# Gated values kept patch by patch, and the w_in matmuls of a step run over all four quarters

## The chip, the cores and the metric

One Trainium2 chip, one core. The metric is the device time of one launch in microseconds (us); the kernel before has a median of 3460.51 us over 3 runs (3444.41 to 3466.08). TensorE is called PE (its weight loads PEld), VectorE DVE, ScalarE ACT, GpSimd POOL, SyncE SP. All data is fp32. SBUF holds 128 partitions; PSUM has 8 banks of 512 fp32 words in each.

## The reference

The input is x of 32 images, 32 channels, 96 x 96 pixels. The program is two parts, one after the other:

```python
x = x + experts(groupnorm(x))      # gate picks 3 of 6 experts an image; each: 3x3 depthwise conv, relu, 3x3 depthwise conv
x = x + fft_conv(groupnorm(x))

def fft_conv(x, w_in, dw_k, fft_filter, w_out):
    x = einsum('oc,bchw->bohw', w_in, x)          # 32 -> 170 channels
    xp = 8x8 patches of x                          # 144 patches an image
    x = irfft2(rfft2(xp) * fft_filter)             # per channel, inside each patch
    y = depthwise 3x3 conv(x, dw_k)                # across patch borders too
    y1, y2 = y[:, :85], y[:, 85:]
    return einsum('oc,bchw->bohw', w_out, gelu(y1) * y2)
```

Only the second part (from about 1180 us of the profile on) is touched by the change.

## The kernel before, in words

**Layout.** In the second part an image lies as 4 quarters of rows (q = 0 to 3) of 32 channels on the 128 partitions. Its 144 patches are 36 to a quarter. After w_in a patch's 64 pixels are on 64 partitions and there are two halves h (partitions 0 to 63 and 64 to 127) that hold different channels: `hidden_patches` (U) is [128, 88 channels, 144 patches]. The filter and the 3x3 kernel are folded, once, into tables of 64 x 64 for each channel (`channel_tables`, line 965), so the FFT, the filter and the convolution are matmuls of one channel's table with its 144 patches.

**Two stages an image.** The main loop (lines 1314 to 1328 for PE, 1382 to 1398 for DVE, 1192 to 1208 for ACT) has for each image k a *first stage* and then eight *sets*.

The first stage has NW = 9 steps. In step v, PE does w_in of image k for 4 patches of each quarter (`w_in_step`, line 1234, matmuls at line 1245: 32 calls of 32 rows x 64 columns, moving 88; the quarter picks the array's row group and PSUM bank 4 + q, h picks the column half) and then w_out of image k - 1 (`w_out_step`, line 1299, matmuls at line 1309: 16 calls of 128 rows x 32 columns, moving 128). Each matmul call shows as two matmul and two weight-load records, since fp32 is done in two passes. w_in goes by pairs of quarters: pair 0 into banks 4 and 5, then pair 1 into banks 6 and 7. ACT copies each pair out to U (`w_in_copy`, line 1148, copies at line 1153) and frees its banks for the same pair of the next step (semaphores `s_w`, `s_we[pair]`). DVE transposes the gated values of image k - 1 in 32 x 32 blocks so that channels lie on partitions (`transposes`, line 1359, two instructions of 128 x 512 at line 1369), and adds the result of w_out of the step before to the image (`residual`, line 1380). The `channels_first` buffers and the PSUM banks of w_out (2 and 3) are double.

The eight sets hold 3, 3, 3, 3, 3, 3, 2, 2 slots of channel pairs. For set S PE runs `border(S+2)` (line 1263), `hidden(S)` (line 1280, the patch's own part) and `add_neighbours(S)` (line 1295, what comes over the patch borders, brought by DMAs from `border` to `neighbours`, lines 1076 and 1190). ACT then takes `gelu` of one half of the channels (line 1180) and DVE multiplies it with the other half into `gated` (`gate`, line 1356), once for the even and once for the odd slots (odd = 0, 1). `hidden(S+1)` writes the same PSUM banks 0 to 3, so it waits for both gates of set S (`need(pe, s_m, 2 * S)`, line 1270). Each engine runs its queue in the program's order.

**`gated`** (gt, line 967) is [128, 44 slots, 144 patches]. A gate of 3 slots writes 3 runs of 144 adjacent words; a transpose reads 32 slots of one patch, with a step of 144 words from element to element, patch after patch.

Four older pieces of code serve as measures. Line 252 copies `taps` tables to SBUF with a step of 32 words from element to element of its inner loop; line 249 copies `tables` with a step of 54 words; line 1347 (and 1174 on ACT) writes `channel_tables` with a step of 128 words. Line 554 (first convolution of the experts) has 24 matmul calls of 32 rows x 64 columns that run over four row groups and two column halves in the innermost loops, moving 288; line 568 (second convolution) has 12 calls of 128 rows x 32 columns over four column groups, moving 288.

The instruction memory is refilled by DMA while the program runs; the page's DMA queue 8, kind "instruction", has 586 packets and 9.60 MB.

Of the kernel before, what the change touches and what calls it, by code (L numbers as in the profile page):

```python
# [13 lines left out]
P = 128  # L14
# [825 lines left out]
NQUAD = 4  # L840
# [107 lines left out]
def filter_part(nc, x1, norm2, w_in, dw_k, filt, w_out, out):  # L948
# [9 lines left out]
    with ExitStack() as ctx:  # L958
        def sb(name, shape):
            return ctx.enter_context(nc.sbuf_tensor(name, shape, F32))  # L960
# [3 lines left out]

        tbl = sb("channel_tables", [P, NCH, 2 * NV])
        U = sb("hidden_patches", [P, NCH, NPC])
        gt = sb("gated", [P, NT4, NPC])
        be = [sb(f"border{i}", [P, RUN + 2 * EDGE]) for i in range(2)]
        bd = [sb(f"neighbours{i}", [P, RUN]) for i in range(2)]
        ct = [sb(f"channels_first{i}", [P, 2 * 512]) for i in range(2)]  # L970
# [53 lines left out]
        def need(eng, s, value):  # L1024
            if value > 0:
                eng.wait_ge(s, value)
# [184 lines left out]
        def _(pe):  # L1211
# [19 lines left out]
                                  mid[half(h), j:j + n, NCH * g:NCH * g + NCH], start=True, stop=True)  # L1231
                    last.then_inc(s_x, 1)

            def w_in_step(k, v, pair):

                if v == 0 and pair == 0:
                    pe.wait_ge(s_xn, k + 1)
                need(pe, s_we[pair], NW * k + v)
                if k == 0 and v == 0:
                    pe.wait_ge(s_xe[pair], NGX)  # L1240
                for i in range(WSTEP):
                    for q in (2 * pair, 2 * pair + 1):
                        cq = slice(C * q, C * q + C)
                        for h in range(2):
                            last = MM(ps[half(h), 4 + q, i * NCH:(i + 1) * NCH], xn[cq, (WSTEP * v + i) * NV:(WSTEP * v + i + 1) * NV], wi[cq, NCH * h:NCH * h + NCH],  # L1245
                                      start=True, stop=True)
                last.then_inc(s_w, 1)

            def border(S):

# [63 lines left out]
            for k in range(B + 1):  # L1314
                for v in range(NW):
                    if k < B:
                        w_in_step(k, v, 0)
                        w_in_step(k, v, 1)
                    if k > 0:
                        w_out_step(k - 1, v)  # L1320
                if k < B:
                    border(NSETS * k)
                    border(NSETS * k + 1)
                    for s in range(NSETS):
                        if s + 2 < NSETS:
                            border(NSETS * k + s + 2)
                        hidden(NSETS * k + s)
                        add_neighbours(NSETS * k + s)

        @block.vector  # L1330
        def _(dve):
# [17 lines left out]
            def gate(S, odd):  # L1349
                k, s = divmod(S, NSETS)  # L1350
                n = SETS[s]
                dve.wait_ge(s_g, 2 * S + odd + 1)
                if s == 0:
                    need(dve, s_te, NW * k)
                o = gt.rearrange("p (t s) n -> p t s n", s=2)[:, CUT[s]:CUT[s + 1], odd, :]
                TT(o, gl[odd][:, 0:n * NPC].rearrange("p (t m) -> p t m", m=NPC),  # L1356
                   ps[:, 2 * odd + 1, 0:n * NPC].rearrange("p (t m) -> p t m", m=NPC), ALU.mult).then_inc(s_m, 1)

            def transposes(k, v):

                j = NW * k + v
                if v == 0:
                    dve.wait_ge(s_m, 2 * NSETS * (k + 1))
                need(dve, s_wo, j - 1)
                t = ct[j % 2].rearrange("p (s q i n) -> p s q i n", s=2, q=NQUAD, i=WSTEP)
                for s in range(2):
                    first = s * (NT4 - SB)
                    g = gt[:, first:first + SB, :].rearrange("p t (q i) -> p q i t", q=NQUAD)[:, :, WSTEP * v:WSTEP * v + WSTEP, :]
                    last = nc.vector.transpose(t[:, s], g)  # L1369
                last.then_inc(s_te, 1)  # L1370

# [57 lines left out]
```

## Time and profile before

| | |
|---|---|
| median of 3 runs | 3460.51 us |
| profiled execution, first to last instruction | 3457.4 us |
| PE matmul busy | 2908.9 us (84%) |
| DVE busy | 1847.5 us (53%) |
| ACT busy | 1311.5 us (38%) |
| mean granted TensorE clock | 0.953 |

The page gives no time for the profiled execution but its span; the median lies 3.1 us above it. Busy times overlap, so no one of them is the time: what counts is which engine waits for which, stage by stage. A granted clock of 1 is 2.4 GHz, 0.5 is 1.2 GHz. In a timeline row "x64" counts records, so 64 matmul records are 32 calls. "Idle before <-issue" is time in which an engine waited for nothing that the profile shows.

### The profile page before, as it was taken

The page shows a single profiled execution, that of the slowest core. Times are in us where ns is not written, and L with a number is a line of the kernel's source. Part 1 is how long each engine was busy: PE and PEld are TensorE (multiplying, and loading weights), DVE is VectorE, ACT ScalarE, POOL GpSimd, SP SyncE. Part 2 cuts the span into 40 slices and gives each one's busy share as a digit, 9 for nine tenths or more (in the row PEclk, how much of TensorE's full clock was granted, in tenths as well). Part 3 has the DMA queues.
Part 4 walks back from the last instruction along what each step waited for, and adds up shares of the span by engine and source line. Part 5 has one row for each costly group of instructions (what it writes and reads, how often), then busy time and mean ns, then how long its engine had stood idle before and what let it go on. Part 6 is the DMA issues. An engine that isn't in the chain of part 4 may idle for free.

```text
span 3457.4 us, 164388 instructions
## 1 busy us (share of the span) xinstructions
PE 2908.9 (84%) x74374; PEld 2020.6 (58%) x74374; DVE 1847.5 (53%) x4198; ACT 1311.5 (38%) x2217; POOL 253.1 (7%) x274
## 2 busy tenths in 40 slices
PE   4699999999996788888888888888888888888887
PEld 4355554555453666666666666666656666666665
DVE  3356565565652245554556555655555555555555
ACT  1234444444342233343434343433433333443332
POOL 2011111111110200000000000000000000000000
PEclk9899999999998599999999999999998999999999
DMA  6578778787764334334443444334433444334433
GB/s 126 124 170 172 164 169 170 172 171 165 165 144 69 32 100 111 95 93 104 117 106 89 107 119 105 89 99 105 116 97 89 105 115 112 89 99 113 113 92 84
DMA packets 451958, 404.16 MB, mean 117 GB/s; under 512 B 404172, under 2 KB 404478, under 8 KB 447497
## 3 DMA queue, kind: packets, MB, share of 16 engines
q1 hardware_dynamic: 446030, 376.93, 47.5%
q10 hardware_dynamic: 5228, 16.70, 1.4%
q8 instruction: 586, 9.60, 1.2%
q14 instruction: 114, 0.93, 0.1%
HBM read 165.77 MB, written 78.16 MB: 71 GB/s over the span
## 4 chain that ended last, share of the span: by engine, by line
PE 49%; DVE 6%; issue 5%; ACT 3%; DMA 3%; ACTq 2%; SPq 1%; POOL 0%; DVEq 0%; POOLq 0%
PE ps L1295 12%; PE ps L1245 10%; PE ps L1280 10%; PE ps L1309 9%; PE ps L1263 8%; DMA neighbours<-border 3%; DVE gated L1356 3%; ACT gelu L1180 2%; DVE channels_first L1369 2%; ACTq L1190 2%; ACT hidden_patches L1153 1%; DVE border L1163 1%; SPq L1052 1%; ACT border L1163 0%; DMA x_normed<-in_L_conv_w_in_dram 0%
## 5 line engine op out<-in xcount | busy, mean ns | idle before, releaser
L1356 DVE TENSOR_TENSOR gated<-gelu,ps 128x432 f32<-128x432 f32 (+1 forms) x512 | 289.3, 567 | 555.8 <-ACT gelu L1180 529.7
L449 ACT ACTIVATE hidden<-ps,hidden_scale 128x576 f32<-128x576 f32 x512 | 351.7, 738 | 614.5 <-PE ps L554 614.5
L1369 DVE STREAM_TRANSPOSE channels_first<-gated 128x512 f32<-128x512 f32 x576 | 571.3, 1043 | 1.1
L1153 ACT COPY hidden_patches<-ps 128x704 f32<-128x704 f32 x576 | 406.5, 749 | 434.3 <-PE ps L1245 434.2
L1280 PE MATMUL ps<-hidden_patches,channel_tables 64*64 64x144 f32 x11264 | 403.4, 287 | 97.4 <-DVE gated L1356 97.4
L1263 PE MATMUL ps<-hidden_patches,channel_tables 64*64 64x144 f32 x11264 | 405.7, 287 | 90.2 <-DVE border L1163 84.8
L568 PE MATMUL ps<-hidden,taps 128*32 128x288 f32 x6144 | 437.3, 417 | 43.1 <-DMA taps<-conv_tables 29.7
L1245 PE MATMUL ps<-w_in_t,x_normed 32*64 32x88 f32 x18432 | 422.3, 259 | 54.2 <-issue 49.3
L1263 PEld LDWEIGHTS ps<-hidden_patches,channel_tables 64*64 64x64 f32 x11264 | 359.4, 134 | 184.6 <-ACT border L1163 114.7
L1163 ACT COPY border<-ps 128x432 f32<-128x432 f32 (+1 forms) x512 | 226.4, 495 | 618.9 <-DVE border L1163 216.9
L554 PE MATMUL ps<-x_rows,taps 32*64 32x288 f32 x12288 | 455.0, 415 | 2.5 <-issue 1.3
L1163 DVE COPY border<-ps 128x432 f32<-128x432 f32 (+1 forms) x512 | 267.9, 565 | 320.1 <-PE ps L1263 160.0
L1245 PEld LDWEIGHTS ps<-w_in_t,x_normed 32*64 32x64 f32 x18432 | 356.7, 145 | 138.8 <-issue 134.4
L1295 PE MATMUL ps<-neighbours,select 64*64 64x432 f32 (+1 forms) x4096 | 400.6, 505 | 43.8 <-DMA neighbours<-border 23.0
L1280 PEld LDWEIGHTS ps<-hidden_patches,channel_tables 64*64 64x64 f32 x11264 | 338.4, 133 | 166.1 <-DVE gated L1356 156.7
L1309 PE MATMUL ps<-channels_first,w_out_t 128*32 128x128 f32 x9216 | 359.2, 296 | 84.9 <-DVE channels_first L1369 68.4
L554 PEld LDWEIGHTS ps<-x_rows,taps 32*64 32x64 f32 x12288 | 271.5, 133 | 179.5 <-issue 94.9
L1180 ACT ACTIVATE gelu<-ps 128x432 f32<-128x432 f32 (+1 forms) x512 | 255.9, 502 | 310.9 <-PE ps L1295 302.7
L1309 PEld LDWEIGHTS ps<-channels_first,w_out_t 128*32 128x32 f32 x9216 | 260.6, 117 | 135.6 <-DVE channels_first L1369 76.8
L790 DVE SCALAR_TENSOR_TENSOR x_image<-ps,out_bias,x_image 128x288 f32<-128x288 f32 x256 | 130.9, 511 | 380.1 <-PE ps L568 378.8
L568 PEld LDWEIGHTS ps<-hidden,taps 128*32 128x32 f32 x6144 | 176.7, 110 | 249.5 <-issue 124.2
L1295 PEld LDWEIGHTS ps<-neighbours,select 64*64 64x64 f32 x4096 | 134.5, 132 | 201.5 <-PE ps L1280 105.4
(147 smaller groups left out, 1328.7 us busy)
## 6 DMA issues: line engine op xcount, KB each, us to landing
neighbours<-border SPq DMA_DIRECT2D x1024, 126.8 KB
taps<-conv_tables SPq DMA_DIRECT2D x192, 216.0 KB
x_image<-in_x_dram SPq DMA_DIRECT2D x128, 288.0 KB, 5.8
x<-x_image SPq DMA_DIRECT2D x128, 288.0 KB, 4.7
x_image<-x SPq DMA_DIRECT2D x384, 96.0 KB
out_dram<-x_image SPq DMA_DIRECT2D x384, 96.0 KB, 2.0
x_rows<-in_x_dram SPq DMA_DIRECT2D x512, 60.0 KB
neighbours<-border ACTq DMA_DIRECT2D x1024, 15.8 KB
```

The lines of the kernel that those rows point to most:

```text
L449: A(hid[T % 3][:, 2 * h:2 * h + 2, :, 1:1 + W], ps1[:, 2 * h:2 * h + 2, 0:XB * W].rearrange("p c (k w) -> p c k w", k=XB), ACT.Relu, scale ...
L554: last = MM(ps1[MP * u:MP * u + MP, f, 0:XB * W], t1s[n % 2][rows, j, dx, :], t[rows, j, u:NBLK:2, dx:dx + W], start=(dx == 0), stop=(dx = ...
L568: last = MM(ps2[RX * f:RX * f + RX, T % 2, 0:XB * W], t2s[n % 2][:, o:o + RX], hid[T % 3][:, f, :, dx:dx + W], start=(dx == 0), stop=(dx = ...
L1153: nc.scalar.copy(o, i).then_inc(s_we[pair], 1)
L1163: last = copy(o[:, i, 0:n, 0:NPR, 0:NPR], ps[:, 4 + i, 0:n * NPC].rearrange("p (u r c) -> p u r c", u=n, r=NPR))
L1245: last = MM(ps[half(h), 4 + q, i * NCH:(i + 1) * NCH], xn[cq, (WSTEP * v + i) * NV:(WSTEP * v + i + 1) * NV], wi[cq, NCH * h:NCH * h + NCH ...
L1263: last = MM(ps[half(h ^ y), 4 + i, o:o + NPC], tbl[half(h), j, NV:2 * NV], U[half(h), j, :], start=True, stop=True)
L1280: last = MM(ps[half(h ^ odd), i, o:o + NPC], tbl[half(h), j, 0:NV], U[half(h), j, :], start=first, stop=True, skip_group_check=not first)
L1295: last = MM(ps[half(h ^ odd), i, 0:n * NPC], sel[half(h ^ y), :], v[half(h ^ y), i, 0:n, 0:NPR, 0:NPR], start=False, stop=True, skip_group ...
L1309: last = MM(o, wo[:, b, s, :], t[:, s, P * q:P * q + P], start=(s == 0), stop=(s == 1), skip_group_check=True)
L1356: TT(o, gl[odd][:, 0:n * NPC].rearrange("p (t m) -> p t m", m=NPC), ps[:, 2 * odd + 1, 0:n * NPC].rearrange("p (t m) -> p t m", m=NPC), AL ...
L1369: last = nc.vector.transpose(t[:, s], g)
```

## The change

`gated` becomes [128, 144 patches, 44 slots]: the 44 slots of a patch are adjacent words. So the gate's inner loop over 144 patches writes with a step of 44 words, while the transposes read 32 adjacent words for each patch. Both have as many elements as before.

`w_in_step` no longer has a pair: one call does all four quarters, with q and h as the innermost loops, so that successive matmul calls go over four row groups and two column halves. It first waits until both pairs of the step before have been copied out. The two increments of `s_w` both come in the last round (i = 3), after q = 1 and after q = 3. The number and shapes of the matmuls and the copies stay the same.

```diff
--- before.py
+++ after.py
@@ -964,7 +964,7 @@
 
         tbl = sb("channel_tables", [P, NCH, 2 * NV])
         U = sb("hidden_patches", [P, NCH, NPC])
-        gt = sb("gated", [P, NT4, NPC])
+        gt = sb("gated", [P, NPC, NT4])
         be = [sb(f"border{i}", [P, RUN + 2 * EDGE]) for i in range(2)]
         bd = [sb(f"neighbours{i}", [P, RUN]) for i in range(2)]
         ct = [sb(f"channels_first{i}", [P, 2 * 512]) for i in range(2)]
@@ -1231,20 +1231,22 @@
                                   mid[half(h), j:j + n, NCH * g:NCH * g + NCH], start=True, stop=True)
                     last.then_inc(s_x, 1)
 
-            def w_in_step(k, v, pair):
-
-                if v == 0 and pair == 0:
+            def w_in_step(k, v):
+
+                if v == 0:
                     pe.wait_ge(s_xn, k + 1)
-                need(pe, s_we[pair], NW * k + v)
-                if k == 0 and v == 0:
-                    pe.wait_ge(s_xe[pair], NGX)
+                for pair in range(2):
+                    need(pe, s_we[pair], NW * k + v)
+                    if k == 0 and v == 0:
+                        pe.wait_ge(s_xe[pair], NGX)
                 for i in range(WSTEP):
-                    for q in (2 * pair, 2 * pair + 1):
+                    for q in range(NQUAD):
                         cq = slice(C * q, C * q + C)
                         for h in range(2):
                             last = MM(ps[half(h), 4 + q, i * NCH:(i + 1) * NCH], xn[cq, (WSTEP * v + i) * NV:(WSTEP * v + i + 1) * NV], wi[cq, NCH * h:NCH * h + NCH],
                                       start=True, stop=True)
-                last.then_inc(s_w, 1)
+                        if i == WSTEP - 1 and q % 2 == 1:
+                            last.then_inc(s_w, 1)
 
             def border(S):
 
@@ -1314,8 +1316,7 @@
             for k in range(B + 1):
                 for v in range(NW):
                     if k < B:
-                        w_in_step(k, v, 0)
-                        w_in_step(k, v, 1)
+                        w_in_step(k, v)
                     if k > 0:
                         w_out_step(k - 1, v)
                 if k < B:
@@ -1352,7 +1353,7 @@
                 dve.wait_ge(s_g, 2 * S + odd + 1)
                 if s == 0:
                     need(dve, s_te, NW * k)
-                o = gt.rearrange("p (t s) n -> p t s n", s=2)[:, CUT[s]:CUT[s + 1], odd, :]
+                o = gt.rearrange("p n (t s) -> p t s n", s=2)[:, CUT[s]:CUT[s + 1], odd, :]
                 TT(o, gl[odd][:, 0:n * NPC].rearrange("p (t m) -> p t m", m=NPC),
                    ps[:, 2 * odd + 1, 0:n * NPC].rearrange("p (t m) -> p t m", m=NPC), ALU.mult).then_inc(s_m, 1)
 
@@ -1365,7 +1366,7 @@
                 t = ct[j % 2].rearrange("p (s q i n) -> p s q i n", s=2, q=NQUAD, i=WSTEP)
                 for s in range(2):
                     first = s * (NT4 - SB)
-                    g = gt[:, first:first + SB, :].rearrange("p t (q i) -> p q i t", q=NQUAD)[:, :, WSTEP * v:WSTEP * v + WSTEP, :]
+                    g = gt[:, :, first:first + SB].rearrange("p (q i) t -> p q i t", q=NQUAD)[:, :, WSTEP * v:WSTEP * v + WSTEP, :]
                     last = nc.vector.transpose(t[:, s], g)
                 last.then_inc(s_te, 1)
```

## Rows read from the trace of the kernel before

**Rows 1.** The page's part 4, the chain that ended last, by engine.

```profile
PE 49%; DVE 6%; issue 5%; ACT 3%; DMA 3%; ACTq 2%; SPq 1%; POOL 0%; DVEq 0%; POOLq 0%
```

**Rows 2.** Timeline, one set of the second part: start, length (us), engine, line, what, [idle before].

```profile
2007.41 1.70 PE L1280 MATMUL ps<-hidden_patches,channel_tables 64*64 64x144 f32 x48 [0.33 <-DVE gated L1356]
2009.20 1.69 PE L1295 MATMUL ps<-neighbours,select 64*64 64x432 f32 x16
2010.22 0.53 ACT L1180 ACTIVATE gelu<-ps 128x432 f32<-128x432 f32 x1 [0.78 <-PE ps L1295]
2010.79 1.35 DVE L1356 TENSOR_TENSOR gated<-gelu,ps 128x432 f32<-128x432 f32 x2 [1.70 <-ACT gelu L1180]
2012.19 0.35 PE L1280 MATMUL ps<-hidden_patches,channel_tables 64*64 64x144 f32 x4 [0.33 <-DVE gated L1356]
```

**Rows 3.** Groups by form: busy us, mean ns | idle before. The gates.

```profile
L1356 DVE TENSOR_TENSOR gated<-gelu,ps 128x432 f32<-128x432 f32 x384 | 231.1, 604 | 387.0 <-ACT gelu L1180 364.4
L1356 DVE TENSOR_TENSOR gated<-gelu,ps 128x288 f32<-128x288 f32 x128 | 58.2, 455 | 168.8 <-ACT gelu L1180 165.3
```

**Rows 4.** Groups by form: VectorE copies whose inner loop writes with a wide step.

```profile
L252 DVE COPY taps<-ps 128x384 f32<-128x384 f32 x8 | 6.4, 804 | 21.4 <-PE ps L585 21.4
L249 DVE COPY tables<-ps 128x480 f32<-128x480 f32 x2 | 2.0, 1006 | 19.9 <-PE ps L580 19.9
L1347 DVE COPY channel_tables<-ps 128x440 f32<-128x440 f32 x6 | 6.3, 1096 | 2.8 <-PE ps L1230 2.6
```

**Rows 5.** Groups by form, the transposes.

```profile
L1369 DVE STREAM_TRANSPOSE channels_first<-gated 128x512 f32<-128x512 f32 x576 | 571.3, 1043 | 1.1
```

**Rows 6.** Timeline, two steps after the last image.

```profile
3439.29 1.95 DVE L1369 STREAM_TRANSPOSE channels_first<-gated 128x512 f32<-128x512 f32 x2
3441.47 1.95 DVE L1369 STREAM_TRANSPOSE channels_first<-gated 128x512 f32<-128x512 f32 x2
```

**Rows 7.** Timeline, one step of a first stage.

```profile
2033.01 1.24 PE L1245 MATMUL ps<-w_in_t,x_normed 32*64 32x88 f32 x64
2033.91 1.39 ACT L1153 COPY hidden_patches<-ps 128x704 f32<-128x704 f32 x2 [0.79 <-PE ps L1245]
2034.18 1.08 PE L1309 MATMUL ps<-channels_first,w_out_t 128*32 128x128 f32 x32
2035.19 1.43 PE L1245 MATMUL ps<-w_in_t,x_normed 32*64 32x88 f32 x64
```

**Rows 8.** Timeline, two issue gaps in a row in a first stage.

```profile
1415.53 0.68 PE L1245 MATMUL ps<-w_in_t,x_normed 32*64 32x88 f32 x23 [0.54 <-issue]
1418.99 0.86 PE L1309 MATMUL ps<-channels_first,w_out_t 128*32 128x128 f32 x24 [0.25 <-issue]
```

**Rows 9.** Stretches: length, busy us (instructions) by engine, clock, DMA, GB/s.

```profile
1396.61:1400.52 3.91, 3.91 (x100) 3.23 (x97) 2.64 (x4) 1.42 (x2) 0.00 (x0) 0.50 0.02 4
1745.39:1770.03 24.64, 21.48 (x868) 17.74 (x865) 21.08 (x29) 13.13 (x20) 0.00 (x0) 1.00 0.26 65
2586.40:2617.65 31.25, 26.90 (x868) 22.30 (x865) 21.25 (x28) 13.17 (x20) 0.00 (x0) 0.78 0.22 54
```

**Rows 10.** Timeline, the first stage of the first image, without w_out.

```profile
1193.81 2.12 PE L1245 MATMUL ps<-w_in_t,x_normed 32*64 32x88 f32 x64 [0.19 <-ACT hidden_patches L1153]
1195.32 1.42 ACT L1153 COPY hidden_patches<-ps 128x704 f32<-128x704 f32 x2 [0.89 <-PE ps L1245]
```

**Rows 11.** Timeline, the turn from one image's sets to the next first stage.

```profile
2023.04 0.96 DVE L1356 TENSOR_TENSOR gated<-gelu,ps 128x288 f32<-128x288 f32 x2 [2.58 <-ACT gelu L1180]
2024.04 3.85 DVE L1369 STREAM_TRANSPOSE channels_first<-gated 128x512 f32<-128x512 f32 x4
2026.09 1.08 PE L1309 MATMUL ps<-channels_first,w_out_t 128*32 128x128 f32 x32 [1.89 <-DVE channels_first L1369]
```

**Rows 12.** Timeline, experts part: four column tiles, then eight tiles.

```profile
601.74 1.66 PE L568 MATMUL ps<-hidden,taps 128*32 128x288 f32 x24
603.33 1.72 PE L554 MATMUL ps<-x_rows,taps 32*64 32x288 f32 x48
```

## The prediction

> **What bounds the kernel now.** I read first the chain of waits: PE carries 49% of it, DVE 6% [rows 1], so what PE waits for decides, stage by stage. The timeline of a set shows a closed loop. `hidden` starts at 2007.41, `add_neighbours` at 2009.20, gelu at 2010.22, the two gates from 2010.79 to 2012.14, the next `hidden` at 2012.19: 4.78 us, and PE's idle time before it is put down to the gate [rows 2]. The border matmuls that lie between don't fill it. In all 224 places where a `hidden` follows a gate within an image, it starts 0.055 us after the second gate ends, as here (2012.14 to 2012.19). So whatever a gate gets longer, the set gets longer.
>
> In the first stage a step has 64 w_in records from 2033.01, 32 w_out records from 2034.18, the next w_in at 2035.19: 2.18 us, PE without a pause. The ACT copies begin 0.90 us after w_in and take 1.39 together [rows 7]. That is PE's own pace, but few steps keep it. The 30 stages with both kinds of matmul last 24.6 (shortest) to 31.3 us (longest) [rows 9], mean 27.2, where 4.15 + 7 x 2.18 + 2.44 = 21.9 would do. Two things take the rest. First, issue gaps: from the gap's end at 1415.53 to that at 1418.99 there are 23 + 32 + 64 + 8 = 127 matmul records, each with a weight load, so 254 instructions in 3.46 us [rows 8]. Such gaps come every 254 or 255 instructions, in this stage alone, which looks like the supply of instructions; at that pace a step's 192 can't take less than 2.62 us. Second, the clock: at a granted 0.50 (1.2 GHz) a step takes 3.91 us [rows 9]. Of the 240 steps after a stage's first, 19 are wholly at that clock, 27 partly (mean 3.06), and of the others the 166 within the stage average 2.65.
>
> **The gate (added cost).** It takes 604 ns for 432 elements and 455 for 288: 1.035 ns each and 157 fixed [rows 3]. With the inner step of 44 words no row shows it. The copies with a wide inner step give, less the same 157: step 32 words (804 - 157)/384 = 1.68 ns, step 54 (1006 - 157)/480 = 1.77, step 128 (1096 - 157)/440 = 2.13 [rows 4]. The lower bound is no cost, 1.035, since those are copies and this has two sources; the upper is 2.13. I take 1.77, of the nearest step. A gate of three slots is then 157 + 432 x 1.77 = 922 ns, of two 667. The second gate now starts 1.35 - 0.60 = 0.75 us after the first (when its gelu is ready) [rows 2, 3]; back to back it would start about 0.10 before the first one's end (two transposes take 1.95, one 1.04) [rows 5, 6], so at 0.82: 0.07 later. A three-slot set grows by 0.07 + 0.32 = 0.39 us. Two-slot gates start 0.96 - 0.455 = 0.51 apart [rows 11]: 0.06 + 0.21 = 0.27. Six such sets and one before the last `hidden` make 2.61 us an image, **+84 us** for 32. The bounds: at 1.035 nothing, at 1.68 +67, at 2.13 +150. DMAs for the neighbours are two sets ahead and only get more time. The skill has a number of its own: the Trainium skill, "Vector Engine (DVE) Microarchitecture Reference", "Measured stream behaviour on trn2", gives 2.50 ns per element for a destination that steps 24 words each element and 1.71 for hops of 4 KiB. By 2.50 the gates would cost an estimated +218 us, by 1.71 about +72; the rows of this kernel lie near the lower one.
>
> **The transposes (gain, mostly covered).** 1043 ns for 512 elements is (1043 - 157)/512 = 1.73 ns each [rows 5], just what the wide steps cost above. With adjacent words I take 1.035: 157 + 530 = 0.69 us, a pair in 1.30 instead of 1.95 to 2.0. Bounds: 0.69 and 1.04. In the steps PE doesn't wait for them. They count in two places. At the turn, w_out of step 0 waits for the first pair with 1.89 us of idle PE [rows 11]: 0.66 less, 0.27 given back by the last gates, 0.39 us an image; some of that is lost again to instruction supply, so 31 x 0.26 = **-8**. After the last image the period is DVE's, 2.18 us [rows 6]; it becomes 2 x 0.6 + 0.3 = 1.5, but PE at 1.2 GHz gives some 1.7: **-5**.
>
> **w_in over four quarters.** 24 calls over eight tiles (1.72 us) take hardly longer than 12 of the same columns over four (1.66) [rows 12]; so eight tiles run side by side, and w_in of 1.17 us (2034.18 - 2033.01 [rows 7]) becomes 0.6. But PE then has nothing to do with it: the last matmul of the quarter pairs is in the eighth round of eight, as pair 0's was before, so the first copy still starts at 0.90, the second ends at 0.90 + 1.39 = 2.29, and now the next w_in waits for both, with some 0.1 us for the semaphore: **2.39 us a step where it was 2.18**. ACT's two copies, once beside the other pair's matmuls, are in series with w_in. So:
> - Warm steps: 73 of the 166 took less than 2.39; lengthening each to 2.39 costs 14 us. Where the supply of instructions sets 2.62 anyway it costs nothing, and a slower step lets it catch up: half, **+7**. The rest stay at 2.65.
> - Steps at 1.2 GHz: the first copy starts 1.51 us after w_in, both take 1.42 [rows 10], 2.98 in all, against 3.91: 19 x 0.93 + 27 x 0.36 = **-28**. Bounds: none of it, or twice, if these stretches shrink or grow.
> - First image (no w_out, 1.2 GHz): its steps of 2.31 (1193.81 to 1196.12, PE already waits for ACT there [rows 10]) become 2.98: 8 x 0.67 = **+5**.
> - The last step of a stage is bounded by the same two copies before and after: nothing.
>
> **Sum.** 84 - 8 - 5 + 7 - 28 + 5 = +55: 3457.4 + 55 = 3512, and 3.1 more for the median, **3516 us** (+1.6%). This case's own range is 3465 (gates at 1.68, the first stages 60 us better) to 3560 (first stages not better at all, gates somewhat dearer).
>
> **Rivals.**
> - *The gaps close.* If the gaps are no limit of pace but come from PE running ahead, PE's pauses for ACT would swallow them: a stage is 3.76 + 7 x 2.39 + 2.44 = 22.9, 4.3 us less than the mean, -129 for 30. With +84 for the gates: 3416, **faster**. It decides if refilling 254 instructions takes less than 2.39 x 254/192 = 3.16 us. For it: the sets, with 192 instructions in 4.78 us, have no such gaps. Against: 3.46 measured with PE waiting [rows 8]. The Trainium skill, "Runtime: NRT & Kernel Launch", "Instruction fetch mechanics", calls crossing a 16 KiB block of instructions mostly hidden; the trace disagrees, with 0.54 and 0.25 us of matmul idle at these two [rows 8]. Chance 0.12.
> - *A wide write is free for a two-source operation.* Gates as before: 3516 - 84 - 4 = 3428. Against: every wide write in the trace is slow. 0.08.
> - *The write costs as with 128 words, or more.* +150 for +84: 3582, and beyond if no row here bounds it. 0.10.
> - *The eight tiles don't run side by side with 88 columns*, since here a round is short (88 of 288 columns): w_in stays at 1.17, the first copy starts at 1.49, the step is 2.98. 166 x 0.33 = 55 instead of 7, and the 1.2 GHz steps gain nothing (+33 against the sum): 3597. 0.07.
> - *The transposes don't get faster*: 3516 + 13 = 3529, inside the forecast.
>
> **Numbers.** The forecast has 0.63. The range 3430 to 3600 leaves out most of the first rival and the far end of the third and fourth. A measurement of this kernel tells 1% from no change, here 3426 to 3495. Faster by more: 0.08 from the first rival and 0.03 from the second. Within: 0.05 from the second, 0.04 from the first, 0.14 from the low side of the forecast. Slower: 0.66.
>
> **What would show it.** Gates of 0.92 and 0.67 us with the next `hidden` still 0.06 behind them and sets of 5.17 us; transposes of 0.69; w_in records done in about 0.85 instead of 1.24; the idle time before w_in released by ACT, steps of 2.39 or more, and gaps still 254 instructions apart, 3.4 us or more. Gates at 0.60, or first stages near 23 us, would make it wrong.

## The result, and the profile after

The changed kernel takes 3545.84 us (median of 4 runs, 3534.48 to 3557.3) where the kernel before takes 3457.55 in the same comparison (4 runs): a ratio of 1.028, interval 1.0235 to 1.0326. That is slower by 88 us; the forecast was 55 slower, 3516 us. The profiled execution spans 3555.3 us, 98 more than the one before, at a mean clock of 0.962. Line numbers moved: w_in is L1246, `border` L1265, `hidden` L1282, `add_neighbours` L1297, w_out L1311, the gate L1357, the transposes L1370.

The page after, its busy times by engine and the chain of waits:

```profile
PE 2839.7 (80%) x74374; PEld 1928.9 (54%) x74374; DVE 1766.8 (50%) x4198; ACT 1310.9 (37%) x2217; POOL 253.0 (7%) x274
PE 29%; DVE 10%; ACT 10%; issue 7%; SPq 6%; DMA 5%; ACTq 1%; POOL 0%; DVEq 0%; POOLq 0%
```

PE and DVE are both busy for less time than before and the kernel is longer; PE's share of the chain fell from 49% [rows 1] to 29%, and DVE and ACT took over. So time went into waits between engines. A set (timeline of the kernel after):

```profile
2132.33 1.70 PE L1282 MATMUL ps<-hidden_patches,channel_tables 64*64 64x144 f32 x48 [0.72 <-DVE gated L1357]
2134.12 1.68 PE L1297 MATMUL ps<-neighbours,select 64*64 64x432 f32 x16
2135.14 0.53 ACT L1180 ACTIVATE gelu<-ps 128x432 f32<-128x432 f32 x1 [0.94 <-PE ps L1297]
2135.70 1.72 DVE L1357 TENSOR_TENSOR gated<-gelu,ps 128x432 f32<-128x432 f32 x2 [2.79 <-ACT gelu L1180]
2137.48 1.21 PE L1282 MATMUL ps<-hidden_patches,channel_tables 64*64 64x144 f32 x32 [1.68 <-DVE gated L1357]
```

The gates end at 2137.42 and `hidden` starts 0.06 later, as in [rows 2]; the two gates take 1.72 us where they took 1.35, and the set 5.15 where it took 4.78. The groups by form of the kernel after (busy us, mean ns | idle before) give the new durations:

```profile
L1357 DVE TENSOR_TENSOR gated<-gelu,ps 128x432 f32<-128x432 f32 x384 | 336.3, 957 | 424.6 <-ACT gelu L1180 424.6
L1357 DVE TENSOR_TENSOR gated<-gelu,ps 128x288 f32<-128x288 f32 x128 | 78.2, 685 | 174.2 <-ACT gelu L1180 174.2
L1370 DVE STREAM_TRANSPOSE channels_first<-gated 128x512 f32<-128x512 f32 x576 | 369.7, 685 | 1.1
L1246 PE MATMUL ps<-w_in_t,x_normed 32*64 32x88 f32 x18432 | 329.4, 258 | 150.6 <-ACT hidden_patches L1153 89.8 <-issue 56.5 <-POOL x_normed L1145 3.2
```

A three-slot gate went from 604 to 957 ns [rows 3], a transpose from 1043 to 685 [rows 5]. PE now idles 89.8 us before w_in for ACT's copies.

The turn, from one image's sets to the next first stage, and the step after it (timeline of the kernel after):

```profile
1479.28 1.01 PE L1246 MATMUL ps<-w_in_t,x_normed 32*64 32x88 f32 x64
1480.62 2.49 DVE L1370 STREAM_TRANSPOSE channels_first<-gated 128x512 f32<-128x512 f32 x4
1481.98 1.08 PE L1311 MATMUL ps<-channels_first,w_out_t 128*32 128x128 f32 x32 [1.69 <-DVE channels_first L1370]
1482.99 1.01 PE L1246 MATMUL ps<-w_in_t,x_normed 32*64 32x88 f32 x64
1483.93 1.08 PE L1311 MATMUL ps<-channels_first,w_out_t 128*32 128x128 f32 x32
1483.97 1.40 ACT L1153 COPY hidden_patches<-ps 128x704 f32<-128x704 f32 x2 [2.32 <-PE ps L1246]
1485.51 1.00 PE L1246 MATMUL ps<-w_in_t,x_normed 32*64 32x88 f32 x64 [0.50 <-ACT hidden_patches L1153]
```

PE waits 1.69 us at the turn for the transposes, where it waited 1.89 [rows 11]. In the step, ACT's copies start 0.98 after w_in and last 1.40, to 1485.37; the next w_in starts at 1485.51, so a step takes 2.52 us with PE idle at its end, where 2.18 was possible [rows 7]. The issue gaps are still there (timeline, further on):

```profile
1862.19 0.83 PE L1246 MATMUL ps<-w_in_t,x_normed 32*64 32x88 f32 x47 [0.50 <-ACT hidden_patches L1153]
1863.78 0.44 PE L1246 MATMUL ps<-w_in_t,x_normed 32*64 32x88 f32 x17 [0.77 <-issue]
```

What these gaps wait for can be read from the DMA packets of queue 8, kind "instruction". The page has 586 of them, each of 16,384 bytes in the trace, for 148,748 matmul and weight-load records: 254 records to a packet, which is the distance from gap to gap. In this trace 94 in 100 of the gaps over 0.3 us end between 1.1 and 1.7 us after such a packet has ended (median 1.4); with packets some 3.7 us apart, chance alone would give about 16 in 100. The next packet starts 1.4 us after the gap's end and takes 1.1 (medians). That makes a round of 3.9 us, the spacing of the gaps. The kernel before shows the same: 94 in 100, and 1.4, 1.3 and 1.1 us. So the gaps are waits for refills of the instruction memory.

The shortest first stage after an image and one of the longest (stretches; columns as in [rows 9]) lie closer together than before, where they were 24.64 and 31.25:

```profile
3388.13:3413.51 25.38, 19.67 (x868) 15.55 (x865) 16.02 (x29) 13.04 (x20) 0.00 (x0) 1.00 0.26 66
1554.95:1583.82 28.87, 21.89 (x869) 17.41 (x865) 16.02 (x29) 13.11 (x20) 0.00 (x0) 0.88 0.24 58
```

To read the runs that follow, all instructions of a trace were sorted into the 31 first stages with both kinds of matmul and the stretches between them (the rest of an image). Means in us; "warm steps" are steps 1 to 7 that lie wholly at a granted 1; "turn wait" is PE's idle time in one turn, and the median of the 31 turns is within 0.02 us of it. The medians are of all runs, the other columns of the one profiled execution, which for the kernel after was the longest of four (3557.3 us).

| kernel | median | first stage | rest of image | turn wait | at 1.2 GHz in first stages, total | warm step, mean |
|---|---|---|---|---|---|---|
| before | 3457.55 | 27.17 | 43.30 | 1.89 | 144 | 2.64 |
| after | 3545.84 | 27.16 | 46.26 | 1.69 | 63 | 2.82 |
| layout alone | 3519.14 | 26.36 | 46.49 | 1.47 | 68 | 2.70 |
| w_in order alone | 3499.67 | 27.94 | 43.46 | 2.15 | 97 | 2.85 |
| gates alone | 3576.73 | 28.07 | 46.22 | 2.14 | 186 | 2.66 |
| transposes alone | 3405.07 | 25.42 | 43.39 | 1.21 | 24 | 2.66 |
| early transposes | 3401.01 | 25.24 | 43.30 | 0.97 | 22 | 2.66 |
| later w_out | 3396.69 | 25.08 | 43.35 | 0.46 | 23 | 2.71 |
| half of the copies | 3536.27 | 26.08 | 46.62 | 1.70 | 62 | 2.69 |
| less w_out, on after | 3609.56 | 27.05 | 48.06 | 1.70 | 710 | none |
| less w_out, on transposes alone | 3339.55 | 22.29 | 44.56 | 1.21 | 413 | 1.93 |

So the 98 us of span are, in the main, the rest of 32 images, 32 x 2.96 = 95 (the last image's alone is 4.9 longer, 2 more than the others'), and the first image's stage, 27.42 for 21.58, +6. What runs before the second part took 1 us more. The first stages of the other images are unchanged as a sum, and the work after the last image's matmuls is 5.2 us shorter (20.6 for 25.7). That the stages are unchanged is two things that cancel, which the experiments separate.

### The profile page after: what moved, and what is told of

Its sections match the earlier page's. It is cut to its first block, busy times and chain, and to the rows that moved or that the text cites. A ratio compares the mean times of both kernels' runs of the same rounds, so it can differ in the third digit from the quotient of the medians.

```text
span 3555.3 us, 164645 instructions
## 1 busy us (share of the span) xinstructions
PE 2839.7 (80%) x74374; PEld 1928.9 (54%) x74374; DVE 1766.8 (50%) x4198; ACT 1310.9 (37%) x2217; POOL 253.0 (7%) x274
## 4 chain that ended last, share of the span: by engine, by line
PE 29%; DVE 10%; ACT 10%; issue 7%; SPq 6%; DMA 5%; ACTq 1%; POOL 0%; DVEq 0%; POOLq 0%
PE ps L1282 8%; DVE gated L1357 8%; PE ps L1246 8%; ACT hidden_patches L1153 7%; PE ps L1297 6%; DMA neighbours<-border 5%; SPq L1076 4%; PE ps L1311 4%; PE ps L1265 3%; ACT gelu L1180 3%; DVE channels_first L1370 1%; ACTq L1190 1%; SPq L1058 1%; DVE border L1163 1%; SPq L1052 1%
## 5 line engine op out<-in xcount | busy, mean ns | idle before, releaser
L1357 DVE TENSOR_TENSOR gated<-gelu,ps 128x432 f32<-128x432 f32 (+1 forms) x512 | 414.5, 889 | 598.8 <-ACT gelu L1180 598.8
L1282 PE MATMUL ps<-hidden_patches,channel_tables 64*64 64x144 f32 x11264 | 407.7, 289 | 166.2 <-DVE gated L1357 166.2
L1265 PE MATMUL ps<-hidden_patches,channel_tables 64*64 64x144 f32 x11264 | 404.9, 286 | 99.6 <-DVE border L1163 85.1
L1282 PEld LDWEIGHTS ps<-hidden_patches,channel_tables 64*64 64x64 f32 x11264 | 342.1, 134 | 251.3 <-DVE gated L1357 251.3
L1265 PEld LDWEIGHTS ps<-hidden_patches,channel_tables 64*64 64x64 f32 x11264 | 359.9, 134 | 193.8 <-ACT border L1163 111.7
L1246 PE MATMUL ps<-w_in_t,x_normed 32*64 32x88 f32 x18432 | 329.4, 258 | 150.6 <-ACT hidden_patches L1153 89.8
L1297 PE MATMUL ps<-neighbours,select 64*64 64x432 f32 (+1 forms) x4096 | 406.7, 512 | 46.9 <-DMA neighbours<-border 26.8
L1311 PE MATMUL ps<-channels_first,w_out_t 128*32 128x128 f32 x9216 | 342.5, 286 | 77.4 <-DVE channels_first L1370 59.3
L1246 PEld LDWEIGHTS ps<-w_in_t,x_normed 32*64 32x64 f32 x18432 | 266.2, 138 | 243.8 <-issue 129.1
L1370 DVE STREAM_TRANSPOSE channels_first<-gated 128x512 f32<-128x512 f32 x576 | 369.7, 685 | 1.1
L1311 PEld LDWEIGHTS ps<-channels_first,w_out_t 128*32 128x32 f32 x9216 | 251.4, 114 | 120.4 <-DVE channels_first L1370 66.4
L1381 DVE TENSOR_TENSOR x_image<-ps,x_image 128x256 f32<-128x256 f32 x288 | 122.2, 424 | 348.6 <-PE ps L1311 346.7
```

What stands on the lines that cost most here:

```text
L1265: last = MM(ps[half(h ^ y), 4 + i, o:o + NPC], tbl[half(h), j, NV:2 * NV], U[half(h), j, :], start=True, stop=True)
L1282: last = MM(ps[half(h ^ odd), i, o:o + NPC], tbl[half(h), j, 0:NV], U[half(h), j, :], start=first, stop=True, skip_group_check=not first)
L1297: last = MM(ps[half(h ^ odd), i, 0:n * NPC], sel[half(h ^ y), :], v[half(h ^ y), i, 0:n, 0:NPR, 0:NPR], start=False, stop=True, skip_group ...
L1311: last = MM(o, wo[:, b, s, :], t[:, s, P * q:P * q + P], start=(s == 0), stop=(s == 1), skip_group_check=True)
```

## Experiments

**Each half of the change alone.** `layout` makes the change to `gated` alone: the declaration, the gate's output view and the transposes' input view, with w_in by pairs. `order` makes the change to `w_in_step` and its call alone. Both are the parts of the diff shown above. From here on a difference in us is against the kernel before as it was timed beside each run: 11 runs, with medians of 3463.42 us for these two and the next two, 3457.81 for `early`, `half_copies` and the two with less w_out, and 3463.64 for the rest.

> The patch-by-patch layout alone (gates write with a step of 44 words, transposes read adjacent words), w_in in two pairs as before. Theory 1 (the gates carry the loss, because each set is a closed loop through the gate): gates 957 and 685 ns, sets 5.18 us apart instead of 4.78, so 2.7 us x 32 = +86 us; the shorter transposes give back about 10 at the turn and after the last image; 3458 + 76 = 3534 us. Theory 2 (the loss comes from w_in over four quarters, whose copies are now in series with it): this kernel is about 10 us faster than before, 3448. First stages near 26.7 us in theory 1.

> w_in over all four quarters alone, gated values slot by slot as before. Theory 1: w_in in 0.95 us instead of 1.17 but a floor of 2.51 us a step instead of 2.18 (first copy 0.97 after w_in, 0.64 + 0.75 for the copies, 0.14 until the next w_in); since instruction supply already makes the mean step 2.65, the 31 first stages together change by -20 to +30 us, the first image's gets 6 us longer: 3440 to 3495. Theory 2: +80 us or more, 3540. Gates 604 ns, sets 4.78 us apart in both.

`layout`: 3519.14 us, ratio 1.0151 (1.0114 to 1.0187), +56. `order`: 3499.67, ratio 1.01 (1.0066 to 1.0133), +36. They add up to 92 against 88 for both. For `layout` 3534 had been expected; `order` came out just above the 3440 to 3495 expected. PE at the turn, in `layout` and in `order`:

```profile
1473.51 1.08 PE L1309 MATMUL ps<-channels_first,w_out_t 128*32 128x128 f32 x32 [1.47 <-DVE channels_first L1369]
```

```profile
2045.96 1.94 PE L1311 MATMUL ps<-channels_first,w_out_t 128*32 128x128 f32 x32 [2.15 <-DVE channels_first L1370]
L1246 PE MATMUL ps<-w_in_t,x_normed 32*64 32x88 f32 x18432 | 334.2, 261 | 147.7 <-ACT hidden_patches L1153 87.8 <-issue 55.8 <-POOL x_normed L1145 3.2
```

The new order is not a small gain but a cost. Its w_in is done earlier, so PE waits longer at the turn (2.15 for 1.89), and w_out there then runs its 32 records in 1.94 us instead of 1.08, at the lower clock.

**Each half of the layout alone.** The memory stays the same, only one of the two views changes.

```diff
# gate_only: the gates write with a step of 44, the transposes read with 144
+ gt = sb("gated", [P, NPC, NT4])
+ o = gt.rearrange("p n (t s) -> p t s n", s=2)[:, CUT[s]:CUT[s + 1], odd, :]
+ old = gt.rearrange("p n t -> p (n t)").rearrange("p (t n) -> p t n", t=NT4)
# transposes_only: the gates as before, the transposes read adjacent words
+ new = gt.rearrange("p t n -> p (t n)").rearrange("p (n t) -> p n t", t=NT4)
```

> Only the gates write with a step of 44 words; the transposes read the same memory with a step of 144 words as before (so they take wrong values), w_in as before. Theory 1: the whole loss and a little more: +86 us, 3544; first stages as before, 27.2 us mean; transposes still 1043 ns. Theory 2: no change.

> Only the transposes read adjacent words (wrong values, since the gates write slot by slot as before), w_in as before. Theory 1: 685 ns each instead of 1043, but off the path except at the turn (0.65 us x 31, part of it lost to instruction supply) and after the last image (5 us): -10 to -25 us, 3433 to 3448. If the transposes were a limit in the steps, the first stages would fall below 25 us and the time below 3400.

`gate_only`: 3576.73 us, ratio 1.0307 (1.0267 to 1.0348), +113. `transposes_only`: 3405.07, ratio 0.9834 (0.9806 to 0.9862), -58. They add up to +55, the layout's +56. Both went further than expected (+86, and -10 to -25), because of the turn, as the rows below show. The turn in `gate_only` (timeline) and the five microseconds from 2075 (stretch):

```profile
2075.91 1.93 PE L1309 MATMUL ps<-channels_first,w_out_t 128*32 128x128 f32 x32 [2.14 <-DVE channels_first L1370]
2075.00:2080.00 5.00, 4.09 (x112) 3.48 (x116) 4.72 (x6) 0.71 (x2) 0.00 (x0) 0.66 0.00 0
```

The turn in `transposes_only` and the steps behind it:

```profile
2005.33 2.49 DVE L1370 STREAM_TRANSPOSE channels_first<-gated 128x512 f32<-128x512 f32 x4
2006.69 1.08 PE L1309 MATMUL ps<-channels_first,w_out_t 128*32 128x128 f32 x32 [1.21 <-DVE channels_first L1370]
2007.70 1.24 PE L1245 MATMUL ps<-w_in_t,x_normed 32*64 32x88 f32 x64
2008.88 1.08 PE L1309 MATMUL ps<-channels_first,w_out_t 128*32 128x128 f32 x32
2009.88 1.24 PE L1245 MATMUL ps<-w_in_t,x_normed 32*64 32x88 f32 x64
```

After 2.14 us of idle PE the clock averages 0.66 over those five microseconds; after 1.21 w_out stays at its 1.08 and the next step takes 2.18 (2007.70 to 2009.88). Over the 31 stages, time at 1.2 GHz is 24 us against 144, step 0 takes 3.46 against 4.47 and step 1 2.18 against 3.06. In kernels with w_in by pairs, waits of 1.21, 1.47, 1.89 and 2.14 go with 24, 68, 144 and 186 us at 1.2 GHz, in 4, 14, 23 and 25 of the 31 stages; with the new order, 1.69 and 2.15 with 63 and 97, in 17 and 23.

**The transposes' rate, or the wait at the turn?** `early` keeps the old layout and its slow transposes, but DVE does those of slots 0 to 31 for steps 0 and 1 before the gates of the last set.

```diff
+ def early_transposes(k):
+     dve.wait_ge(s_m, 2 * (NSETS * k + 6))
+     need(dve, s_wo, NW * k)
+     for v in range(2):
+         transpose_part(k, v, 0)
  # DVE's loop over the sets, ahead of the gates of the last one
+ if s == NSETS - 2:
+     early_transposes(k)
  # (not shown: in the first stage, steps 0 and 1 then transpose slots 12 to 43 alone)
```

> The kernel before with two transposes moved: the ones that read slots 0 to 31 for the steps 0 and 1 of the first stage run on VectorE in its pause before the gates of the last set (those slots are complete by then). All else as before. Theory 1 (PE's wait at the turn from the sets to the first stage costs twice: itself, and by the drop of the granted clock to 0.5 that follows it): the turn's idle time falls from 1.9 to about 0.9 us, step 0 from 4.47 to about 3.2, hardly any first stage at 1.2 GHz; 3463 - 65 = 3398 us. Theory 2 (the clock falls for other reasons): only the wait itself, 31 us or less: 3432 to 3450.

3401.01 us, ratio 0.984 (0.981 to 0.9869), -57. Its transposes by form, and w_out at the turn:

```profile
L1364 DVE STREAM_TRANSPOSE channels_first<-gated 128x512 f32<-128x512 f32 x576 | 578.6, 1053 | 1.1
2000.95 1.08 PE L1309 MATMUL ps<-channels_first,w_out_t 128*32 128x128 f32 x32 [0.97 <-DVE channels_first L1364]
```

With transposes of 1053 ns the gain is that of transposes of 684 ns. After the last image the faster ones save 5.6 us of their 58 (the work there takes 20.2 us for 25.7), `early` 1.7. In the first stages their rate is worth nothing beyond the turn (warm steps take 2.66 us in both kernels and 2.64 before); the wait at the turn, with the clock behind it, is worth all of it.

**Give PE something else to do at the turn.** `late` issues w_out one step later on PE, so that w_in of steps 0 and 1 come ahead of the first w_out. `late_early` has both edits.

```diff
-                    if k > 0:
-                        w_out_step(k - 1, v)
+                    if k > 0 and v > 0:
+                        w_out_step(k - 1, v - 1)
+                if k > 0:
+                    w_out_step(k - 1, NW - 1)
```

> The kernel before with PE's order in the first stage changed alone: w_out follows one step later (w_in 0, w_in 1, w_out 0, w_in 2, w_out 1, ...), all else as before, the transposes too. PE then has w_in of step 1 to do where it waited 1.9 us for the transposes. Theory 1 (that wait also brings the drop of the clock): idle time at the turn about 0.5 + 0.2 us in two pieces, hardly any first stage at 1.2 GHz, and the last two w_out cover ACT's last copies; first stages 25.0 instead of 27.2, 3458 - 68 = 3390 us. Theory 2 (clock independent of the wait): 31 x 1.3 = 40 us less at most, 3418.

> Both the later w_out and the two early transposes. If supply of instructions sets the first stages once the wait and the clock are out of the way, little more comes: 24.5 to 25 us a stage, 3375 to 3400 us, within 15 us of either alone. If the wait still counted, the two would add: 3340.

`late`: 3396.69 us, ratio 0.9805 (0.9776 to 0.9834). `late_early`: 3393.59, ratio 0.9805 (0.9773 to 0.9837): the second edit adds nothing that shows in the time, though time at 1.2 GHz in the first stages falls from 23 us to 7. Both beat both kernels. The turn in `late`:

```profile
2006.56 1.24 PE L1245 MATMUL ps<-w_in_t,x_normed 32*64 32x88 f32 x64
2007.46 1.39 ACT L1153 COPY hidden_patches<-ps 128x704 f32<-128x704 f32 x2 [0.33 <-PE ps L1245]
2007.64 3.92 DVE L1371 STREAM_TRANSPOSE channels_first<-gated 128x512 f32<-128x512 f32 x4
2008.26 1.48 PE L1245 MATMUL ps<-w_in_t,x_normed 32*64 32x88 f32 x64 [0.46 <-ACT hidden_patches L1153]
2009.72 1.08 PE L1309 MATMUL ps<-channels_first,w_out_t 128*32 128x128 f32 x32
```

PE idles 0.46 us, for ACT, and w_out follows without a wait.

**Are the issue gaps a limit of pace?** `half_copies` is the changed kernel in which ACT, from image 1 on, copies out 2 of 4 patches of each quarter, so the floor of ACT's two copies is gone.

```diff
+            w = WSTEP if k == 0 else 2
# and w in place of WSTEP in the output and input views of the copy
```

> The changed kernel, but from the second image on ACT copies only 2 of the 4 patches of each quarter out of PSUM after w_in (half of the copying is left out). The floor of a step falls from 2.51 to about 1.95 us, PE's own pace. Theory 1 (the supply of instructions sets the mean step at 2.62 or more and the serial copies add only where they lie between two gaps): steps without a drop of clock 2.65 us on average instead of 2.82, first stages 25.8 instead of 27.2, 3546 - 43 = 3503 us. Rival (the serial copies are the whole limit, gaps close by themselves): first stages about 20 us, 3546 - 215 = 3330 us.

3536.27 us, ratio to before 1.0224 (1.0182 to 1.0266). The median is only 10 us below that of the kernel after, where 43 were expected. In the profiled executions, 24 us apart, the first stages are 1.08 us shorter each (26.08 us; 25.8 expected), 33 in all, and the rest of an image is 0.36 longer, 11 in all. w_in by form in `half_copies`:

```profile
L1247 PE MATMUL ps<-w_in_t,x_normed 32*64 32x88 f32 x18432 | 332.3, 257 | 113.7 <-issue 97.9 <-ACT hidden_patches L1154 12.2 <-POOL x_normed L1145 3.2
```

ACT's 89.8 us of idle time before w_in fell to 12.2, and issue's rose from 56.5 to 97.9. The shortest step is 1.95 us, the mean warm one 2.69. Gaps inside bursts: 145 with 171 us, against 127 with 105 in the kernel after. They still come 253 or 254 instructions apart, half of them 3.92 us or more after the one before, 5 in 100 under 3.48. So the gaps are a limit of pace of their own: with the wait for ACT nearly gone they grow from 0.83 to 1.18 us each.

**The same from the side of demand.** Only 4 of the 16 calls of w_out in each step, on the kernel after and on `transposes_only`, so a step has 144 instructions instead of 192.

```diff
-  for b in range(2):
-      for s in range(2):
-          for q in range(NQUAD):
+  for q in range(NQUAD):    # b = 0, s = 0
```

> The changed kernel with 4 of the 16 w_out matmul calls a step (the rest left out): 144 instructions a step instead of 192, weight loads included. Supply at 3.46 us for 254 instructions would need 1.96 us a step, less than the floor of 2.51. Theory 1: the gaps in PE's issue disappear from the first stages and steps are 2.51 almost throughout, first stages about 24 us. Rival (gaps have another cause and come once or so in a step whatever the count): steps stay near 2.8.

> The kernel before with transposes that read adjacent words (wrong values) and 4 of the 16 w_out matmul calls a step: nothing but supply should hold a step above 1.65 us (PE 1.45, VectorE 1.6, ACT's two copies 1.4). Theory 1: steps average 1.96 us or more with gaps still 254 instructions apart, first stages 18.5 to 20 us. Rival (no limit of supply): steps of 1.65, first stages 16 us.

One run each: 3609.56 us and 3339.55. A step of the first (timeline), and its PEclk line:

```profile
2243.17 1.52 PE L1246 MATMUL ps<-w_in_t,x_normed 32*64 32x88 f32 x64 [0.92 <-ACT hidden_patches L1153]
2244.68 1.39 ACT L1153 COPY hidden_patches<-ps 128x704 f32<-128x704 f32 x2 [1.65 <-PE ps L1246]
2246.21 1.52 PE L1246 MATMUL ps<-w_in_t,x_normed 32*64 32x88 f32 x64 [0.94 <-ACT hidden_patches L1153]
PEclk9899999999996877888778887788877888778887
```

Less work takes 64 us longer. Each step has 0.9 us of idle PE, the clock goes to 1.2 GHz and stays there through the stage (710 us in all), and at that clock w_in and the two copies take 3.04 us a step, where 2.51 was expected. So the first stages are as long as with all of w_out, 27.05 us for 27.16. The loss lies behind them: the sets begin at the low clock (229 us at 1.2 GHz in the rest of the images, 35 in the kernel after), and the rest of an image takes 48.06 us for 46.26, 56 us in all. Demand is 144 instructions in 3.04 us, and of 127 gaps 4 are left. In the second kernel (timeline):

```profile
2203.03 1.24 PE L1245 MATMUL ps<-w_in_t,x_normed 32*64 32x88 f32 x64
2204.20 0.43 PE L1307 MATMUL ps<-channels_first,w_out_t 128*32 128x128 f32 x8
2204.73 1.18 PE L1245 MATMUL ps<-w_in_t,x_normed 32*64 32x88 f32 x48
2206.34 0.53 PE L1245 MATMUL ps<-w_in_t,x_normed 32*64 32x88 f32 x16 [0.44 <-issue]
```

a step can take 1.70 us (2203.03 to 2204.73), and gaps are back, 30 of them, 254 or 255 instructions and 3.77 us (median) apart. Its first stages take 22.29 us, not the 18.5 to 20 expected, with 413 us at 1.2 GHz; the 79 steps free of that take 1.93 on average. So gaps are there where PE's own pace would use 254 instructions in 3.0 us (144 in 1.70) or 3.3 (192 in 2.51), and nearly gone where it uses them in 5.4 (144 in 3.04). No run lies between.

**The step of the gate's write.** Both on the kernel after: gates from image 1 on write elsewhere in `gated`, with a step of 24 or, in `step45`, of 45 words.

```diff
+ if k > 0:
+     o = gt_all[:, 0:NPC * 24].rearrange("p (n t) -> p t n", t=24)[:, 2 * (CUT[s] % 8) + odd:2 * (CUT[s] % 8) + odd + 2 * n - 1:2, :]
```

> The changed kernel, but from the second image on the gates write with a step of 24 words instead of 44 (values land in wrong places). By the rows of the kernel before (1.68 to 2.13 ns an element for steps of 32, 54, 128 words, 1.85 measured for 44) 950 ns for 432 elements; by the Trainium skill's 2.50 ns for 24 words, 1237 ns.

> The changed kernel, but from the second image on the gates write with a step of 45 words, so that every other element starts at an odd word (values land in wrong places). If the cost is that each element lies in another line of memory: 950 ns, as at 44. If it depends on the step's size or parity: something between 750 and 1240.

One run each: 3723.77 us and 3550.97. The gates of `step24`, then of `step45`, by form:

```profile
L1360 DVE TENSOR_TENSOR gated<-gelu,ps 128x432 f32<-128x432 f32 x384 | 439.6, 1252 | 435.1 <-ACT gelu L1181 435.1
L1360 DVE TENSOR_TENSOR gated<-gelu,ps 128x288 f32<-128x288 f32 x128 | 102.1, 893 | 185.8 <-ACT gelu L1181 185.2
```

```profile
L1360 DVE TENSOR_TENSOR gated<-gelu,ps 128x432 f32<-128x432 f32 x384 | 335.3, 957 | 424.9 <-ACT gelu L1181 424.9
```

The mean of 1252 contains the 12 such gates of the first image at 957; without them it is (384 x 1252 - 12 x 957)/372 = 1262, and the step of 24 words costs (1262 - 157)/432 = 2.56 ns an element. A step of 45 costs the same 1.85 as 44, so this odd step is no cure. The time follows the gates: a set takes 5.73 us for 5.18, the kernel 178 us more.

## Why the prediction was right, and where it was not

The sign, the range and the bounding argument held. The measured 3545.84 us lies near the range's far end for the reasons named there, first stages not better at all and gates somewhat dearer. Single terms did not hold, and two of them missed in opposite directions by more than their bounds.

- **The gates: right.** 922 and 667 ns forecast, 957 and 685 measured, (957 - 157)/432 = 1.85 ns against the 1.77 taken. The second gate starts 0.80 us after the first (0.82 forecast), `hidden` 0.06 behind the last, a set takes 5.18 us (5.17). In the sets of an image that is 2.7 us, 86 in all against 84; the table has 2.96 for the rest of an image, and the other 0.26 was not isolated (time at 1.2 GHz there went from 14 to 35 us). The whole is +113 when done alone: with gates of 957 ns and slow transposes the turn wait grows to 2.14 us and its stages lengthen by 0.9, which the term had left out. The Trainium skill, "Vector Engine (DVE) Microarchitecture Reference", "5.2 Measured stream behaviour on trn2", has 2.50 ns for a destination stepping 24 words; `step24` agrees with 2.56, but 44 and 45 words measure 1.85, so that figure doesn't carry over to them, and its 1.71 for 4 KiB hops is nearer but low.
- **The transposes: the rate right, the term too small by a factor of four.** 0.69 us forecast, 0.685 measured. The term of -8 - 5 = -13 priced the shorter wait at the turn as a wait alone. Measured alone it is -58. Of the 27.17 - 25.42 = 1.75 us that a stage gains, the wait itself is 0.68; the rest fits the clock, 120 us less at 1.2 GHz. At the 3.91 us of a step there [rows 9] against 2.64 that is an estimated 120/3.91 x 1.27 = 39 us or 1.26 a stage, 1.94 together, a little more than the 1.75. The text had counted the 46 slow steps as given, and asked neither what made them slow nor which part of the change moves it. `early` shows that the wait is the cause, with transposes as slow as before.
- **w_in over four quarters: the mechanism right, the sum of the wrong sign.** +7 - 28 + 5 = -16 forecast, +36 measured alone. The floor is 2.51 us, not 2.39: the copies start at 0.97, not 0.90, and the wait behind them is 0.14, not 0.1. w_out starts 0.95 after w_in, not 0.6 (the 64 records start within 0.77 us; from [rows 12] I had taken twice the rate of four tiles). More costly was "where the supply of instructions sets 2.62 anyway it costs nothing": warm steps went from 2.64 to 2.85, 178 of them, +37 us against the forecast's +7. Removing the floor in `half_copies` gives 2.69, as much as `layout`, which has w_in by pairs and 2.70, against 2.82 in the kernel after. So floor and gaps add for the most part: of the 0.33 us by which the floor lies above 2.18, warm steps show 0.21. The gain at 1.2 GHz was there but smaller: 97 us for 144, an estimated 47/3.91 x 1.27 = 15 (the prediction's 28 is 27.4 by its own terms). The turn wait grew by 0.26, 8 us, since w_in ends earlier while DVE does not; that was not in the sum. The first image cost 5.8, forecast 5.
- **The tail: right.** 5.2 us less in the kernel after, -5 forecast; the last steps are 1.52 us apart, 1.5 to 1.7 forecast.
- **How it came out close.** Forecast +84 - 13 - 16 = +55, measured alone +113 - 58 + 36 = +91. In the first stages the slower step took back what the higher clock gave, and the errors, +29, -45 and +52, partly cancel. That the sum is off by 33 us, less than two of its three terms, is luck. (The prediction counts 30 first stages in places and 31 in others; there are 31.)
- **The rivals.** *The gaps close*: refuted. They stay in `half_copies`, where PE waits 78 us less for ACT, and are gone where the demand per microsecond falls. The Trainium skill, "Runtime: NRT & Kernel Launch", "Instruction fetch mechanics", calls the crossing of a block mostly hidden. Over the whole kernel that holds, with 127 gaps for 586 packets; the first stages are where it doesn't, with 0.83 us for each gap. *A wide write is free*: refuted by 957 ns. *As with 128 words or more*: refuted for 44 words, 1.85 against 2.13 ns; a step of 24 words would have been dearer still. *Eight tiles not side by side*: half true, 0.95 us is nearer to 1.17 than to 0.6, and the floor came out at 2.51, not 2.98, because the copies still start at 0.97, not at 1.49. *Transposes no faster*: refuted.

What stays open: why floor and gaps add, that is why a stage whose pace is set by refills doesn't absorb 0.33 us of waiting in each step. The spacing of gaps barely moved (median 3.93 before, 3.95 after; the slowest 5 in 100 from 4.28 to 4.66). The traces show where the time goes: warm steps 1, 2 and 3 take 2.18, 2.39 and 2.53 us in `layout` and 2.52, 2.55 and 2.78 in the kernel after, 0.75 us more together, while steps 4 to 7 differ by 0.33 together. So most of it lies early in a stage, where gaps are still few; why later gaps don't make up for it was not isolated. Also not tried: the later w_out together with the new layout or the new order of w_in.

## What to carry to other kernels

Find the closed loop between engines first; there a longer instruction costs its full difference, while an instruction that got faster off the loop is worth only what it takes off a wait of the bounding engine. Price such a wait of PE with the clock behind it: sort the stages by the wait ahead of them, and see how long the steps after it ran at 1.2 GHz. And before merging two half-buffers' work into one call, ask what the first half used to hide: here ACT's copies ran beside the other pair's matmuls. Moving w_out back by one step in PE's queue, with nothing else changed, took 67 us off.

## What was unexpected in the hardware's behaviour

- A PE wait of 1.21 us at the turn left w_out at 1.08 us for its 32 records; after waits of 2.14 and 2.15 it took 1.93 and 1.94 in the turns shown, and with the order of w_in unchanged the total at 1.2 GHz rises with the wait.
- Leaving out three quarters of w_out made the changed kernel slower, 3609.56 us for 3545.84 (one run). In the first stages the low clock took back what the missing work gave, with w_in at 1.52 us instead of 1.01, and the sets behind them, begun at the low clock, took 56 us more.
- A DVE write with a step of 24 words costs 2.56 ns an element, one of 44 or 45 words 1.85, adjacent ones 1.035. There is no simple rule of the step: from 24 to 44 words the cost falls, and in the copies of [rows 4] it rises from 1.68 at 32 words to 2.13 at 128. An odd step, 45, costs what 44 does.
- PE's stops every 254 instructions follow the instruction packets: they end 1.4 us (median) after a packet of 16,384 bytes has ended, 94 in 100 of them within 1.1 to 1.7.
- 64 records of 32 x 64 with 88 columns over eight tiles take 1.01 us from start to end, over four at a time 1.24; with 288 columns eight tiles had doubled the rate of four [rows 12].
